# Perceiver cross attention: turned probabilities moved into the key projection, and the first group's outputs between the first scores

## The reference, cut to what matters

```python
xn = layer_norm(ctx); ln_lat = layer_norm(latents)        # latents: (4, 256, 256)
q = ln_lat @ Wq                                           # 16 heads of 64
k, v = split(concat([xn, ln_lat], 1) @ Wkv)
weight = einsum('bhld,bhnd->bhln', q * scale, k * scale)
weight = where(concat([mask, ones]), weight, -max)        # mask: which keys count
out = einsum('bhln,bhnd->bhld', softmax(weight), v)
x = x + out.reshape(b, l, 1024) @ Wout
```

## Time and profile before

| what | us |
|---|---|
| median of the three runs | 2274.18 |
| lowest and highest | 2271.08, 2274.73 |
| the profiled execution's own time | 2274.03 |
| its span, first to last instruction | 2272.2 |
| PE busy | 2110.1 |
| DVE busy | 1704.8 |
| ACT busy | 1338.1 |
| POOL busy | 494.2 |

### The profile page before, as it was taken

The page is one execution under the profiler, slowest core; times in us unless marked ns, Lnnn a source line. Parts: engine busy times, 40 slices in busy tenths (PEclk is TensorE's granted clock), DMA queues, the critical chain, the costliest instruction groups (busy, mean ns, idle before and its releaser), DMA issues.

```text
span 2272.2 us, 49686 instructions
## 1 busy us (share of the span) xinstructions
PE 2110.1 (93%) x16354; PEld 1711.6 (75%) x16354; DVE 1704.8 (75%) x4834; ACT 1338.1 (59%) x3908; POOL 494.2 (22%) x274
## 2 busy tenths in 40 slices
PE   3899999999997757899999999999999999999986
PEld 3677877877875435788888888888888888888875
DVE  5777676676673557889888978897889788988872
ACT  1667466566563015567666766676667666766661
POOL 2111011011100012323222322232223222322210
PEclk9999999999998878899999999999999999999998
DMA  3000000000000400011111111111111111111000
GB/s 113 6 11 1 6 11 1 6 11 1 19 12 12 137 0 11 13 45 36 32 50 50 31 33 50 50 31 33 50 48 33 33 50 46 36 31 50 13 13 21
DMA packets 47107, 70.12 MB, mean 31 GB/s; under 512 B 9078, under 2 KB 33828, under 8 KB 46628
## 3 DMA queue, kind: packets, MB, share of 16 engines
q1 hardware_dynamic: 44516, 62.34, 9.0%
q10 hardware_dynamic: 2368, 4.98, 0.6%
HBM read 50.54 MB, written 1.05 MB: 23 GB/s over the span
## 4 chain that ended last, share of the span: by engine, by line
PE 55%; issue 2%; ACT 2%; DVE 1%; DMA 1%; POOL 0%; SPq 0%; DVEq 0%; ACTq 0%; POOLq 0%
PE ps_loc L1559 17%; PE ps_loc L1665 10%; PE ps_loc L1636 7%; PE ps_loc L1675 5%; PE ps_loc L1598 4%; PE ps_loc L1609 4%; PE ps_loc L1625 4%; PE ps_loc L1578 3%; DMA late<-y_all 1%; ACT prob_loc L1806 0%; PE ps_loc L1647 0%; DMA w_raw<-in_ffn_Wqkv_dram 0%; PE ps_loc L1542 0%; ACT L1838 0%; POOL rnorm L2289 0%
## 5 line engine op out<-in xcount | busy, mean ns | idle before, releaser
L2289 POOL TENSOR_TENSOR rnorm<-norm_floor,half_loc 128x32 f32<-128x32 f32 x48 | 302.4, 6301 | 620.1 <-DVE norm_floor L1979 498.2
L1559 PE MATMUL ps_loc<-w_high,xT 128*128 128x512 f32 x1152 | 379.1, 410 | 5.4 <-DVE w_low L1968 3.8
L1806 ACT ACTIVATE prob_loc<-prob_loc,top_loc 128x128 f32<-128x128 f32 x768 | 298.4, 398 | 39.8 <-DVE top_loc L2043 36.8
L1665 PE MATMUL ps_loc<-xnT_loc,w 128*128 128x256 f32 (+1 forms) x1056 | 252.7, 385 | 2.4 <-DVE kT_loc L2109 1.2
L658 ACT ACTIVATE prob<-prob,new_top 128x256 f32<-128x256 f32 x512 | 252.1, 496 | 0.0
L1559 PEld LDWEIGHTS ps_loc<-w_high,xT 128*128 128x128 f32 x1152 | 204.7, 189 | 55.7 <-issue 11.8
L2043 DVE CUSTOM_DVE_ANT_0 prob_loc<-ps_loc,const,rnorm 128x128 f32<-128x128 f32 x768 | 218.9, 345 | 27.1 <-PE ps_loc L1598 25.4
L840 DVE CUSTOM_DVE_ANT_0 prob<-ps_cross,bias 128x256 f32<-128x256 f32 x512 | 185.0, 420 | 67.3 <-PE ps_cross L440 52.8
L1798 ACT ACTIVATE qT_loc<-ps_loc 128x512 f32<-128x512 f32 x96 | 57.4, 598 | 302.1 <-PE ps_loc L1578 302.1
L1559 PE MATMUL ps_loc<-w_low,xT 128*128 128x512 f32 x576 | 228.4, 397 | 0.0
L1665 PEld LDWEIGHTS ps_loc<-xnT_loc,w 128*128 128x128 f32 (+1 forms) x1056 | 191.4, 190 | 28.9 <-DVE kT_loc L2109 2.4
(11 more groups left out here) (184 smaller groups left out, 4324.8 us busy)
## 6 DMA issues: line engine op xcount, KB each, us to landing
w_raw<-in_ffn_Wqkv_dram SPq DMA_DIRECT2D x24, 512.0 KB, 5.4
v_mid<-v_loc SPq DMA_DIRECT2D x48, 256.0 KB, 3.6
w_raw<-in_ffn_Wqkv_dram SPq DMA_DIRECT2D x24, 256.0 KB, 4.0
wo<-in_ffn_Wo_dram SPq DMA_DIRECT2D x24, 256.0 KB, 3.7
w<-in_ffn_W_dram SPq DMA_DIRECT2D x12, 341.0 KB, 4.0
w<-in_ffn_W_dram SPq DMA_DIRECT2D x6, 640.0 KB, 5.2
ctx_raw<-in_ctx_dram SPq DMA_DIRECT2D x12, 256.0 KB, 2.6
w<-in_ffn_W_dram SPq DMA_DIRECT2D x12, 256.0 KB
```

The costliest lines, as they stand in the source:

```text
L1559: ins = pe.matmul(ps[:, DENSE + j % 2, :], xT[:, px, kk, t * P:(t + 1) * P], wqkv[pw][:, kk, col:col + 512], start=kk == 0 and n == 0, sto ...
L1665: ins = pe.matmul(ps[0:n, DENSE + m % 2, part * T:(part + 1) * T], w1[:, kk, col:col + n], xnT[:, kk, :], start=kk == 0, stop=kk == KD - 1)
L1806: ins = act.activation(pr, pr, ACT.Exp, bias=top[:, h, t:t + 1], scale=-1.0, accum_out=total[:, h, t:t + 1])
L2289: pool.tensor_tensor(rnorm[:, b % 2, t, :], norm2_floor[:, :], half[:, :], ALU.pow).then_inc(rnorm_done, 8)
```

## The change

In `keys`, `turn_probs` of the unit before stands behind each of the four key parts, for pairs 0 to 3, in place of pairs 0 and 1 ahead of parts 2 and 3; the wait for `lat_done` moves from before part 2 to behind part 0. In `attend`, PE does the outputs of group 0 between the scores of pairs 1 and 2, group 1 between `turn_probs` 4 and 5, and the rest as in the diff. ACT and DVE follow with their own orders: ACT copies pair 1 before key part 2 and pair 3 before the parts of the next chunk; DVE does the minima of pairs 0 to 3 and the running minimum, then the copies of pairs 4 and 5 together, minima 4 and 5, and then copies and minima of 6 and 7 in turn. The same computation is done.

```diff
                 pe.wait_ge(w_split, KD)
                 for j in range(4):
-                    if j == 2 and last is not None:
-                        pe.wait_ge(lat_done, min(turn + 1, B))
-                    if j >= 2 and last is not None:
-                        turn_probs(last, j - 2)
                     if j < 2:
                         free(j)
...
                     ins.then_inc(k_full, U // 4)
+                    if last is not None:
+                        if j == 0:
+                            pe.wait_ge(lat_done, min(turn + 1, B))
+                        turn_probs(last, j)
...
                 pe.wait_ge(x_done, turn * 2)
                 scores(u, 0)
                 scores(u, 1)
-                for g in range(1, 4):
-                    turn_probs(last, 2 * g)
-                    scores(u, 2 * g)
-                    scores(u, 2 * g + 1)
-                    turn_probs(last, 2 * g + 1)
-                    weigh(last, g - 1, turn)
+                weigh(last, 0, turn)
+                scores(u, 2)
+                scores(u, 3)
+                turn_probs(last, 4)
+                weigh(last, 1, turn)
+                turn_probs(last, 5)
+                scores(u, 4)
+                scores(u, 5)
+                turn_probs(last, 6)
+                scores(u, 6)
+                scores(u, 7)
+                turn_probs(last, 7)
+                weigh(last, 2, turn)
                 weigh(last, 3, turn)
...
             def attend(u, last, turn, uc=None):
                 probs_out(last, 0)
+                probs_out(last, 1)
                 keys_out(u, 2)
-                probs_out(last, 1)
+                probs_out(last, 2)
                 keys_out(u, 3)
-                probs_out(last, 2)
+                probs_out(last, 3)
                 if uc is not None:
                     copy_parts(u, uc)
-                probs_out(last, 3)
...
-                    for pair in range(PAIRS):
+                    dve.wait_ge(bias_done, uc)
+                    for pair in range(ON_ACT):
                         probs_out(last, pair)
-                        if pair == 0:
-                            dve.wait_ge(bias_done, uc)
                         minima(u, pair, bias[:, :])
-                        if pair == 3:
-                            running(ch, u, 0)
+                    running(ch, u, 0)
+                    probs_out(last, 4)
+                    probs_out(last, 5)
+                    minima(u, 4, bias[:, :])
+                    minima(u, 5, bias[:, :])
+                    probs_out(last, 6)
+                    minima(u, 6, bias[:, :])
+                    probs_out(last, 7)
+                    minima(u, 7, bias[:, :])
                     running(ch, u, 1)
```

## The result

The changed kernel takes 2289.69 us (median of six runs) against 2273.69 us for the kernel before, a ratio of 1.0076 with a 95% interval of 1.0063 to 1.0088: slower by 16.0 us. The forecast was 2289 us, slower.

What follows compares the result with a forecast made beforehand. PE was taken to set the pace, busy for 93% of the span. 15 steps x 0.95 us plus 1.0 us for the moved wait made 15.2 us, so 2274.0 became 2289 us; range 2274 to 2297.

Steps and rivals of the forecast that it cites:

- The walk: Cross step, PE and DVE timed from first scores to turning of the next input: 20.84 against 21.64, +0.95 us a step.
- T5: PE's turning of pair 5's probabilities: would start at 8.64, waits 1.13 us for DVE, second half 0.1 more.
- S7: PE's scores of pair 7: due at 14.82, but at 15.14 for pair 5's minima, a wait of 0.32 us.
- M4: DVE's minima of pair 4: at 12.24 in the walk, 1.34 us after that pair's scores start.
- P4: DVE's two copies of pair 4's turned probabilities out of PSUM: at 9.02, behind pair 3's minima and the running minimum.
- the ledger: Cross step's terms: -0.30 forms, -0.43 old hole before fourth scores, +1.23 T5, +0.43 S7, making +0.93 us.
- The forms: PE's changes between full and split array forms: 0.30 us saved a step (0 to 0.60), a direct change taken as 0.15.
- Kept at nothing: Keys block: PE's turned probabilities wait for ACT's copies by 0 us, with 1.6 us of slack at the first.
- The moved wait: PE's earlier wait for DVE's next latents, first step after the first two batch changes: net +0.5 us, twice.
- B: Rival, chance 0.13: gain and new wait about cancel, DVE's copy half a us sooner; 0.15 a step, 2277 us.
- C: Rival, chance 0.13: PE waits for nobody, each step gains 0.73 us; 2264 us.
- D: Rival, chance 0.08: more gaps and transposes in a row lower the granted clock; 2.6 us a step, some 2328 us.

## Why the prediction was right, point by point

- **The walk.** Predicted from S0: T5 at 9.77, S4 at 10.9, S6 at 13.85, S7 at 15.14, W2 at 17.23, N at 20.84. Measured in the step above (S0 at 335.19): 9.76, 10.94, 13.94, 15.32, 17.41, 21.01. T5's wait is 344.95 - (341.95 + 1.88) = 1.12 us against 1.13. That step is one of the longer ones, since M4 comes late in it (347.61, 1.48 after S4); in the step from 153.96, of 38.37 us, N comes at 20.88. The steps between ordinary starts are 38.34 to 38.55, mostly 38.35, against 37.37: +0.98 with +0.95 predicted. That P4's place on DVE causes it is shown by a dose either way: 1.10 us earlier takes 1.11 off the step, later adds 0.63, another engine takes 1.28 off. With T5 at 1.28 in place of 1.23 the ledger gives -0.30 - 0.43 + 1.28 + 0.43 = 0.98, the measured step.
- **The forms.** The unknown, a direct change, was taken as one way (0.15). The rows of after show SS to W 1.93 (335.19 to 337.12) and W to SS 1.88 (337.12 to 339.00), the same as from SS or W to T. So a direct change costs what leaving for the full form costs, and the bound of 0 is out. The Trainium skill, "TensorEngine Tiling (Array Packing)", Key Properties, says that a change of tiling mode drains the TensorE, and gives no price; these rows agree with it if 64\*128 and 128\*64 are taken as two modes. Returns of T's weight load after "issue" fell from 91 to 48. I had said 60: four a step, but T5's own is counted as a wait for DVE, so three.
- **Kept at nothing.** The keys take 9.25 us in the step above, as walked; T1 to T3 don't wait for ACT there. In the first step of the first batch T1 waits 0.17 us for ACT, which I had not seen: its keys take 86.53 - 76.73 = 9.80 us, 0.55 more than the others'.
- **The moved wait** has the right size, but more than it makes the first steps longer. From the first keys to S0 the first step of batch 2 takes 296.47 - 285.77 = 10.70 us, against 288.89 - 280.49 = 8.40 before. Without a wait the two T moved there make 1.75 of that, so the wait's net is 0.55, and 0.58 in batch 3, with 0.5 predicted; T0 comes 2.81 us after K0 where I had 2.62. The whole first steps last 40.17 and 39.80 against 38.28 and 38.25 before: 1.89 and 1.55, so 0.91 and 0.57 beyond the 0.98 of every step. The first batch's first step has 0.55 more too (38.89 against 37.36), all of it in its keys. Together +2.0 in place of +1.0. Most of the second us is these 0.55 and 0.36 behind S0 in batch 2, two places that the sum did not have. In batch 2 M4 begins 1.71 us after S4's start, where the walk had 1.34, and S6 waits 0.22. What delays M4 there is open. The two fences show S0 of batch 2's first step, in the kernel before and in the changed one.

```profile
288.89 2.00 PE L440 MATMUL ps_cross<-kT,qT 64*128 64x256 f32 x16
```

```profile
296.47 2.00 PE L440 MATMUL ps_cross<-kT,qT 64*128 64x256 f32 x16
```

- **The sum.** 15 x 0.98 + 2.0 = 16.7 us by the steps, 15.2 predicted, 16.0 in the medians. The tables have 16.3 for fourteen steps alone, with 0.5 us in a few steps that lose more than 0.98, so some 17.3 for all. That the total came out within 1 us of 2289 is in part luck: the trace's steps lost some 2 us more than forecast, and the medians of the kernel before, taken at different times, lie between 2272.0 and 2273.7.
- **The rivals.** B and C fell with T5's wait. What C supposed, a free T5, is made by the experiments with P4 on ACT and before the minimum: the change is then worth -0.13 to -0.30 us a step, less than C's 0.73, since S7 still waits in both and C had given back that wait as well. D did not happen at waits of 1.05 us, but falls of the clock came with waits of 1.68 to 2.04, each 3.4 us long and worth 1.2 to 1.3 us, where D had 6.8 and 2.6.

## What to carry to other kernels

Where one engine sets the pace, the work between two of its operations can hide what another engine does for the second of them. Moving that work away uncovers the other engine. Before such a move, walk that engine's queue from the first operation that changes its time to the copy that frees the next buffer, with start-to-start times from the trace. Then fill the hole from both sides: put the freeing copy ahead of work that nobody waits for yet, or on an idle engine, and put independent work of the pacing engine where the other one is slow. A step's length in the trace settles a tenth of a microsecond where the medians of whole runs, 7 us apart at their ends, need many runs.

## What the runs showed of the hardware that was not expected

The time between the cross attention and the layers is not fixed. In these profiles the stretch from the last matmul of the cross attention to the first of the layers took 115.9 us before and 111.0 us in the changed kernel, with the same work and mean clocks of 0.80 and 0.84. That is 4.9 us, a third of the effect studied, and it went the other way. It is no trait of the changed kernel: over the eleven profiles of this case the time from the start of the last output projection to the first matmul of the layers lies between 117.7 and 125.1 us, at mean clocks between 0.85 and 0.80. The granted clock also fell to 0.50 in steps otherwise at 1.00, for 3.4 us, behind five of fifteen waits of 1.68 to 2.04 us of PE (those of 1.81 and 1.84 were not among the five), and never in a step of the changed kernel, whose longest wait for T5 is 1.1 us. In the first step, before any wait of T5, it is low for some 3 us in four of the eleven profiles. Which property of the work before them brings these falls about was not tried.
